# Decays in SBUF in a ring of five, with two state places, doubled PSUM banks and a joint silu trip, in the mix block of a two-layer kernel

## The chip, the core and the metric

The kernel runs on one core of a Trainium2 chip. The engines are PE (TensorE, matmuls), DVE (VectorE), ACT (ScalarE), POOL (GpSimd) and SP, which issues most of the DMAs. SBUF and PSUM are the core's memories; PE writes its sums to PSUM only. The metric is the device time of one execution in microseconds, less is better.

## The reference

Two layers on x of 8 sequences with 512 tokens of 256 channels. The first adds attention and a mixture of experts; the second, which is what the change touches, adds a state-space block (Mamba) and a linear layer on quantised data:

```python
xn = _layernorm(x, axis=-1)
x = x + _L1_attn_ref(xn, ...) + _L1_ffn_ref(xn, ...)

# _L1_attn_ref, per sequence, D_INNER 512, D_STATE 16
x, z = jnp.split(in_proj(hidden), 2, axis=-1)
u = jax.nn.silu(conv4(x) + conv1d_b)
dt_low, B_var, C_var = split(u @ x_proj_w.T)
delta = jax.nn.softplus(dt_low @ dt_proj_w.T + dt_proj_b)
dA = jnp.exp(delta[..., None] * A)
dBu = delta[..., None] * B_var[:, :, None, :] * u[..., None]
h = dA * h + dBu                      # over the 512 steps
y = einsum('bdn,bn->bd', h, c) + u * D_param
out = (y * jax.nn.silu(z)) @ out_proj_w.T

# _L1_ffn_ref: x and weight rounded to a 6 bit grid in blocks of 32
out = xd @ wd.T + bias
```

## The kernel before

Three blocks run one after another: `route_block` sends tokens to experts, `attend_block` does attention and experts, `mix_block` the second layer. The change is in `mix_block`, which occupies the last 1200 us.

There a sequence (a batch, b = 0 to 7) is cut into 32 **pieces**, numbered n over all batches, 256 in all. A piece is a quarter of the states of 64 channels on 128 partitions, laid out as two halves of 512 steps, so 1024 elements per partition. Eight pieces (`PER_CHUNK`) are one chunk of 128 channels. A piece n goes through four engines:

- ACT, `decay`: two exponentials of 512 elements (line 1333). They write into a **state place** in PSUM, `state(n)`, two banks; there are three places, used in turn. It waits until the read of piece n - 3 has emptied the place.
- POOL, `drive`: a product of 1024 elements, `rep` times `bc`, from SBUF into a ring `work` in SBUF with `WS` = 8 slots (line 1192). It waits until PE has summed the piece that was in the slot.
- DVE, `scan` (line 1460): a `tensor_tensor_scan` with the decay from PSUM and the drive from SBUF. It overwrites the decay with the states. Then `read` (line 1466) multiplies the states by C, back into the slot of `work`. DVE's order is scan n, side tasks, read n - 1.
- PE, `sum_states`: eight matmuls for each pair of pieces, into the bank `YB` of PSUM (line 1584). `seed` starts each chunk's sum with u * D, and waits until `gate_y` on DVE (line 1474) has multiplied the chunk before by silu(z) out of the same bank.

The order of all work is written by hand. Beside the pieces of batch b each engine has **side tasks** for the next batch f = b + 1, placed at piece numbers by the tables `PE_AT`, `ACT_AT`, `DVE_AT`, `POOL_AT`: the normalised tokens are turned, projected with four taps (line 1559) and passed through silu (1276), quantised by POOL and DVE (lines 1154, 1440, 1443, 1164, 1166, 1171), B, C and delta are made (1567, 1571, softplus 1304 and 1306), z is made (1552, silu 1314), and POOL forms the scans' inputs (1177, 1179), gathers the experts' outputs for batch b + 2 (1130) and adds them (1136). All side results pass through one PSUM bank, `TB`. The out-projection of batch b - 1 (1591 to 1595) stands among them at pieces 2 to 6. In the first batch they come `LATE` = 5 pieces later.

Every engine takes its instructions in this order, and a wait holds up all behind it. ACT must load a table whenever it changes between the functions exp, ln and silu (ACT_TABLE_LOAD). SP sends the delta and drive rows through HBM to have them copied across partitions (`store_inputs`, `load_inputs`, `load_quad`, `store_rows`).

Of the kernel before, what the change touches and what calls it, by code (L numbers as in the profile page):

```python
# [9 lines left out]
ALU = mybir.AluOpType  # L10
ACT = mybir.ActivationFunctionType
AX = mybir.AxisListType

P = 128
# [42 lines left out]
WS = 8  # L57
# [10 lines left out]
PE_AT = {"turn_x": (0, 1), "out": (2, 3, 5, 6), "w": 1, "first_quant": (2, 3), "x": (7, 9, 11, 13), "bc": 16, "dt": (18, 19, 20, 21),  # L68
         "z": (22, 23, 24, 25), "turn_quant": (26, 27)}
ACT_AT = {"normalise": 0, "turned": (1, 2), "out": (5, 8), "w": 2, "first_quant": (3, 4), "x": (10, 12, 14, 16), "silu_u": 16, "step": 9,  # L70
          "rows": 18, "dt": (19, 20, 21, 22), "softplus": 22, "z": (24, 25, 26, 27), "quant": (28, 29), "silu_z": 29, "weigh": 24}
DVE_AT = {"max": 2, "binade": 6, "statistics": 26}
POOL_AT = {"down": 9, "grid": 14, "up": 17, "gather": 23, "add": 27, "input": 28, "root": 31}
FIRST_ACT = {"weigh": 0}
# [855 lines left out]
def mix_block(nc, io, sb):  # L930

    with ExitStack() as ctx:
# [36 lines left out]
        work = buf("work3", [P, WS, 2, SEQ])  # L969
        absmax = buf("absmax", [P, TT * NBLK, 2])  # L970
# [4 lines left out]
        YB, TB = 6, 7  # L975
# [66 lines left out]

        def state(n):
            return ps[:, 2 * (n % 3):2 * (n % 3) + 2, :]

        with nc.Block() as block:
            @block.sync
            def _(sp):
# [49 lines left out]
                for b in range(BATCH + 1):  # L1098
                    if b < BATCH:
                        load_inputs(b, 1)  # L1100
# [3 lines left out]
                    if b < BATCH:  # L1104
                        load_inputs(b, 2)
# [3 lines left out]
                    if b < BATCH:  # L1109
                        load_inputs(b, 3)  # L1110
                    if b + 1 < BATCH:
                        store_rows(b + 1)
# [9 lines left out]
            def _(pool):  # L1122
# [90 lines left out]
                for b in range(BATCH):  # L1213
                    f = b + 1
                    for q in range(PIECES):
                        drive(b, q)
                        if b == 0:
                            if q == FIRST_POOL["add"]:
                                add_experts(1)
                            if q == FIRST_POOL["root"]:  # L1220
                                root(1)
                        if b + 2 < BATCH:
                            if q == POOL_AT["gather"]:
                                pool.drain()
                                place_gather(b + 2)
                                gather(b + 2, range(2))
# [551 lines left out]
```

## Time and profile before

| | us |
|---|---|
| median of 3 runs | 2224.48 (2223.17 to 2225.88) |
| profiled execution, its own time | 2220.31 |
| its span | 2218.5 |
| busy PE, DVE, ACT, POOL | 1719.3, 1488.8, 1004.6, 942.7 |

The span runs from the first instruction to the last. The mix block's pieces lie between 1128 and 2195 us of it. The profile's views used below are: busy time of the engines in a stretch (from:to, length, then busy us and count of instructions for PE matmul, PE weight load, DVE, ACT and POOL, the TensorE clock granted as a share, the DMAs' share, GB/s); groups of instructions by line (line, engine, operation, out<-in, partitions x elements, count | busy us, mean ns | idle us before them and who ended it); the waits (who waited <- for whom, us, times, longest); the timeline (start us, duration us, engine, line, operation, with equal neighbours merged as x2; in square brackets the idle time before and who ended it); and the durations of one line. An engine's instructions may overlap by some hundredths of a us.

### The profile page before, as it was taken

The numbers are of one execution on the slowest core, as the hardware profiler recorded it, in microseconds if no ns is written. First come the engines' busy times: TensorE is split into PE (matmuls) and PEld (weight loads), VectorE is DVE, ScalarE is ACT, GpSimd is POOL, SyncE is SP. The second block draws the span as 40 slices with busy tenths as digits, with TensorE's granted clock in tenths as the row PEclk, the third lists the DMA queues.
The fourth block names the chain that finished last, engine by engine and source line by source line (L and its number), as shares of the span: only waits on it lengthen the run. The fifth ranks groups of instructions, "written<-read, shape, count | busy, mean of one in ns | idle before, by whom it ended". The sixth has DMA issues, their size and how long they took to land.

```text
span 2218.5 us, 21659 instructions
## 1 busy us (share of the span) xinstructions
PE 1719.3 (77%) x6696; PEld 757.2 (34%) x6696; DVE 1488.8 (67%) x1744; ACT 1004.6 (45%) x1542; POOL 942.7 (42%) x676
## 2 busy tenths in 40 slices
PE   7499999999999999994727696685967859677645
PEld 7253535262625353531302141321413224132202
DVE  6446464546464646372068796987979888797995
ACT  3125252525343443434334746556465554656541
POOL 2700000000000000002288786877777877677761
PEclk9899999898989898997858796786977869777756
DMA  4553635262625354423141331423214142231420
GB/s 180 203 88 104 102 103 95 97 108 96 109 96 93 111 79 126 68 51 104 42 159 48 111 118 58 146 84 138 109 59 156 53 152 95 77 133 39 152 86 9
DMA packets 103055, 223.79 MB, mean 101 GB/s; under 512 B 12641, under 2 KB 64994, under 8 KB 99282
## 3 DMA queue, kind: packets, MB, share of 16 engines
q1 hardware_dynamic: 99922, 214.69, 34.1%
q0 software_dynamic: 3072, 8.37, 1.1%
q8 instruction: 28, 0.46, 0.1%
q14 instruction: 33, 0.27, 0.0%
HBM read 169.56 MB, written 53.48 MB: 101 GB/s over the span
## 4 chain that ended last, share of the span: by engine, by line
PE 18%; DVE 16%; issue 8%; ACT 8%; DVEq 1%; DMA 1%; POOLq 1%; POOL 1%; ACTq 0%; SPq 0%
DVE ps L1460 11%; PE ps L1559 9%; DVE work L1466 5%; PE ps L1584 3%; PE ps L1552 2%; ACT ps L1333 2%; PE ps L1571 2%; PE ps L1567 1%; ACT L1333 1%; ACT u L1276 1%; ACT inputs L1304 1%; ACT sz L1314 1%; ACT e_rows L1252 1%; PE ps L1591 0%; ACT L1306 0%
## 5 line engine op out<-in xcount | busy, mean ns | idle before, releaser
L1192 POOL TENSOR_TENSOR work<-rep,bc 128x1024 f32<-128x1024 f32 x256 | 600.2, 2365 | 166.2 <-PE ps L1584 143.1
L1460 DVE TENSOR_TENSOR_SCAN ps<-ps,work 128x1024 f32<-128x1024 f32 x256 | 585.2, 2286 | 119.5 <-ACT ps L1333 119.5
L1333 ACT ACTIVATE ps<-rep,a_neg 128x512 f32<-128x512 f32 x512 | 331.1, 682 | 311.9 <-DVE work L1466 310.1
L708 DVE TENSOR_REDUCE m<-ps 128x1 f32<-128x512 f32 x512 | 328.0, 686 | 158.8 <-PE ps L814 156.0
L631 ACT ACTIVATE prob<-ps 128x1024 f32<-128x1024 f32 x256 | 257.3, 1021 | 224.5 <-PE ps L838 222.7
L1584 PE MATMUL ps<-work,pick 128*32 128x512 f32 x1024 | 182.1, 792 | 180.7 <-DVE work L1466 180.7
L1466 DVE TENSOR_TENSOR work<-ps,bc 128x1024 f32<-128x1024 f32 x256 | 308.6, 1206 | 0.0
L572 POOL TENSOR_TENSOR m_parts<-m,nil 128x16 bf16<-128x16 f32 x32 | 7.0, 220 | 603.2 <-DVE m L708 603.2
L1559 PE MATMUL ps<-xn_t,in_taps 128*128 128x510 f32 (+3 forms) x512 | 232.4, 608 | 8.7 <-ACT x L1322 5.6
L814 PE MATMUL ps<-k_st,q_st 96*128 96x512 bf16 x512 | 200.3, 436 | 30.9 <-DVE m L708 24.7
L838 PE MATMUL ps<-q_st,k_st 99*128 99x512 bf16 x512 | 166.6, 423 | 1.0 <-DVE e_rest L684 0.3
L780 PE MATMUL ps<-rows_t,w 128*128 128x320 f32 x512 | 149.4, 440 | 4.3 <-ACT rows_t L609 4.3
L849 PE MATMUL ps<-prob,v 128*32 128x512 f32 x1024 | 147.5, 650 | 0.1
L1559 PEld LDWEIGHTS ps<-xn_t,in_taps 128*128 128x128 f32 x512 | 96.3, 193 | 146.0 <-issue 131.1
L1552 PE MATMUL ps<-xn_t,in_z 128*128 128x512 f32 x128 | 91.5, 858 | 55.2 <-ACT sz L1310 47.1
L789 PE MATMUL ps<-w,hid 128*128 128x256 f32 x512 | 120.8, 384 | 6.0 <-ACT hid_rest L613 6.0
L1584 PEld LDWEIGHTS ps<-work,pick 128*32 128x32 f32 x1024 | 22.6, 122 | 301.0 <-DVE work L1466 255.4
L586 POOL TENSOR_TENSOR att<-att,x_res 128x1024 f32<-128x1024 f32 x8 | 18.8, 2344 | 244.4 <-DVE att L693 244.4
L814 PEld LDWEIGHTS ps<-k_st,q_st 96*128 96x128 bf16 x512 | 50.2, 101 | 206.8 <-DVE m L708 168.2
L780 PEld LDWEIGHTS ps<-rows_t,w 128*128 128x128 f32 x512 | 97.4, 193 | 41.3 <-ACT rows_t L609 4.7
L680 DVE COPY e_out<-ps 128x256 f32<-128x256 f32 x32 | 12.0, 417 | 144.0 <-PE ps L789 144.0
L612 ACT ACTIVATE hid<-ps 128x256 f32<-128x256 f32 x128 | 49.0, 383 | 128.6 <-PE ps L780 128.6
(176 smaller groups left out, 2087.4 us busy)
## 6 DMA issues: line engine op xcount, KB each, us to landing
rep<-rep_rows SPq DMA_DIRECT2D x128, 512.0 KB, 6.1
w<-in_w SPq DMA_DIRECT2D x32, 1024.0 KB
bc<-bc_rows SPq DMA_DIRECT2D x32, 512.0 KB, 4.0
rep_rows<-inputs SPq DMA_DIRECT2D x32, 512.0 KB, 5.2
qk_parts<-parts SPq DMA_DIRECT2D x96, 128.0 KB
q_st<-qk_parts SPq DMA_DIRECT2D x96, 128.0 KB, 10.4
k_st<-qk_parts SPq DMA_DIRECT2D x96, 128.0 KB, 11.2
dispatch<-zeros SPq DMA_DIRECT2D x4, 1280.0 KB, 10.5
```

The costliest lines, as they stand in the source:

```text
L631: nc.scalar.activation(prob[:, n % PB, :, :], ps[:, ST[n % 2]:ST[n % 2] + 2, :], ACT.Exp, scale=SCALE).then_inc(prob_ready, 1)
L708: nc.vector.tensor_reduce(m[:, g % 2, qt, 2 * pair + i:2 * pair + i + 1], ps[:, S0 + i, :], AX.X, ALU.max).then_inc(s_reduced, 1)
L780: x = nc.tensor.matmul(ps[:, HIDE[i] + h % 2, 0:CAP], w1[:, i, k, h * P:(h + 1) * P], rows_t[:, k, :], start=(k == 0), stop=(k == KD - 1))
L814: nc.tensor.matmul(ps[:, S0 + i, :], q_st[0:STACK, h, qt * P:(qt + 1) * P], k_st[0:STACK, h, :], start=True, stop=True).then_inc(s_done, 1)
L838: x = nc.tensor.matmul(ps[:, ST[n % 2] + i, :], k_st[0:STACK + MROWS, h, kt * P:(kt + 1) * P], q_st[0:STACK + MROWS, h, :], start=True, st ...
L849: x = nc.tensor.matmul(ps[r * VW:(r + 1) * VW, PV, :], v[:, kt, g * GH + r, :], prob[:, (2 * k + r // 2) % PB, r % 2, :], start=(kt == 0), ...
L1192: nc.gpsimd.tensor_tensor(work[:, n % WS, :, :], rep[:, g % RS, 2 * h:2 * h + 2, 1, :], bc[:, k, 0, :].unsqueeze(1).broadcast_to([P, 2, SE ...
L1333: e = nc.scalar.activation(state(n)[:, i, :], rep[:, g % RS, 2 * h + i, 0, :], ACT.Exp, scale=a_neg[:, c, 2 * h + i, k:k + 1])
L1460: nc.vector.tensor_tensor_scan(s, s, work[:, n % WS, :, :].rearrange("p i t -> p (i t)"), 0.0, ALU.mult, ALU.add).then_inc(state_ready, 1)
L1466: nc.vector.tensor_tensor(work[:, n % WS, :, :], state(n), bc[:, k, 1, :].unsqueeze(1).broadcast_to([P, 2, SEQ]), ALU.mult).then_inc(read_ ...
L1559: x = nc.tensor.matmul(ps[:, bank, s:], in_x[:, k, TAPS - 1 - s, c * P:(c + 1) * P], xn_t[:, k, 0:SEQ - s], start=(s == 0 and k == 0), sto ...
L1584: x = nc.tensor.matmul(ps[j * CH:(j + 1) * CH, YB, :], pick[:, :], work[:, n % WS, i, :], start=False, stop=(n % PER_CHUNK >= PER_CHUNK - 2))
```

## The change

- `decay` writes into `decays` in SBUF, a ring of five pieces (`DS`), and waits for the scan of piece n - 5. `scan` reads both its inputs from SBUF and writes the states to PSUM, where there are now two places. It has a third wait, for the read of piece n - 2. `WS` goes from 8 to 7.
- `YB` and `TB` are two PSUM banks each. `seed` waits for the gating of the chunk before last; side tasks alternate between the banks.
- `gate_y` stands three pieces behind the start of the next chunk instead of one.
- silu of z for batch f - 1 follows directly on silu of u for batch f, under one table. The exponential of the softplus stands one piece ahead of its logarithm.
- Side tasks have new positions, written as chains that may begin before their batch (negative numbers); the out-projection moves to pieces 9 to 13, its copies to 15 and 18. SP loads the inputs of all chunks and stores the B and C rows ahead of the output's store.

```diff
-WS = 8
+WS = 7
+DS = 5
...
+GATE = 3
+PE_AT = {"turn_x": (-2, -1), "x": (1, 3, 5, 7), "bc": 11, "dt": (14, 15, 16, 17), "z": (18, 19, 20, 21), "turn_quant": (22, 23)}
+POOL_AT = {"down": 7, "grid": 14, "up": 17, "gather": -11, "add": -5, "input": 25, "root": -1}
+OUT_PROJ, OUT_COPY = (9, 10, 12, 13), (15, 18)
...
+        decays = buf("decays", [P, DS, 2, SEQ])
-        YB, TB = 6, 7
+        YB, TB = (6, 7), (4, 5)
...
+        def chains(n):
+            return [(f, n - (f - 1) * PIECES - (LATE if f == 1 else 0)) for f in range(1, BATCH)]
+
         def state(n):
-            return ps[:, 2 * (n % 3):2 * (n % 3) + 2, :]
+            return ps[:, 2 * (n % 2):2 * (n % 2) + 2, :]
...
                     if b < BATCH:
-                        load_inputs(b, 1)
+                        for c in range(1, DC):
+                            load_inputs(b, c)
+                    if b + 1 < BATCH:
+                        store_rows(b + 1)
...
-                    if n >= 3:
-                        act.wait_ge(read_ready, n - 2)
+                    if n >= DS:
+                        act.wait_ge(state_ready, n - DS + 1)
                     for i in range(2):
-                        e = nc.scalar.activation(state(n)[:, i, :], rep[:, g % RS, 2 * h + i, 0, :], ACT.Exp,
+                        e = nc.scalar.activation(decays[:, n % DS, i, :], rep[:, g % RS, 2 * h + i, 0, :], ACT.Exp,
                                                  scale=a_neg[:, c, 2 * h + i, k:k + 1])
...
+                        if at == ACT_AT["silu_u"]:
                             silu_u(f)
+                            if f > 1:
+                                silu_z(f - 1)
...
                     dve.wait_ge(drive_ready, n + 1)
+                    if n > 1:
+                        dve.wait_ge(read_ready, n - 1)
                     s = state(n).rearrange("p i t -> p (i t)")
-                    nc.vector.tensor_tensor_scan(s, s, work[:, n % WS, :, :].rearrange("p i t -> p (i t)"), 0.0,
-                                                 ALU.mult, ALU.add).then_inc(state_ready, 1)
+                    nc.vector.tensor_tensor_scan(s, decays[:, n % DS, :, :].rearrange("p i t -> p (i t)"),
+                                                 work[:, n % WS, :, :].rearrange("p i t -> p (i t)"), 0.0, ALU.mult, ALU.add).then_inc(state_ready, 1)
...
+                    if n > PER_CHUNK and (n - GATE) % PER_CHUNK == 0:
+                        c = (n - GATE) // PER_CHUNK - 1
+                        gate_y(c // DC, c % DC)
...
-                    if c or b:
-                        pe.wait_ge(y_ready, b * DC + c)
-                    nc.tensor.matmul(ps[:, YB, :], d_diag[:, c, :], u[:, (b * DC + c) % US, :], start=True, stop=False)
+                    if b * DC + c >= 2:
+                        pe.wait_ge(y_ready, b * DC + c - 1)
+                    nc.tensor.matmul(ps[:, YB[c % 2], :], d_diag[:, c, :], u[:, (b * DC + c) % US, :], start=True, stop=False)
```

How the order moves is seen at two places. The first is DVE at the seam of batch 0 and batch 1: before, with scans on line 1460 (printed as SCALAR_TENSOR_TENSOR), reads on 1466 and the gating on 1474:

```order
L1466 TENSOR_TENSOR work<-ps,bc 128x1024 [waits state_ready]
L1460 SCALAR_TENSOR_TENSOR ps<-ps,work 128x1024 [waits drive_ready,decay_ready]
L1474 TENSOR_TENSOR sz<-ps,sz 128x512 [waits z_taken,summed]
L1466 TENSOR_TENSOR work<-ps,bc 128x1024 [waits state_ready]
L1460 SCALAR_TENSOR_TENSOR ps<-ps,work 128x1024 [waits drive_ready,decay_ready]
L1430 TENSOR_REDUCE absmax<-xn 128x32 [waits quant_ready,xn_ready3]
```

The same place with the change, where scans are line 1468, reads 1474 and the gating 1482:

```order
L1468 SCALAR_TENSOR_TENSOR ps<-decays,work 128x1024 [waits read_ready,drive_ready,decay_ready]
L1436 TENSOR_REDUCE absmax<-xn 128x32 [waits quant_ready,xn_ready3]
L1474 TENSOR_TENSOR work<-ps,bc 128x1024 [waits state_ready]
L1468 SCALAR_TENSOR_TENSOR ps<-decays,work 128x1024 [waits read_ready,drive_ready,decay_ready]
L1440 TENSOR_SCALAR absmax<-absmax 128x32
L1442 RECIPROCAL inv_scale<-absmax 128x32
L1474 TENSOR_TENSOR work<-ps,bc 128x1024 [waits state_ready]
L1468 SCALAR_TENSOR_TENSOR ps<-decays,work 128x1024 [waits read_ready,drive_ready,decay_ready]
L1474 TENSOR_TENSOR work<-ps,bc 128x1024 [waits state_ready]
L1468 SCALAR_TENSOR_TENSOR ps<-decays,work 128x1024 [waits read_ready,drive_ready,decay_ready]
L1482 TENSOR_TENSOR sz<-ps,sz 128x512 [waits z_taken,summed]
```

The gating has moved from the second scan of the new batch behind its fourth, the block maxima stand two pieces earlier, and each scan reads `decays` and waits for `read_ready` too.

The second is ACT. Before, at the end of batch 0, the copies of z and of the quantised tokens end in silu of z (line 1314) with a table load on either side:

```order
L1310 ACTIVATE sz<-ps 128x512 [waits z_done] x2
L1318 ACTIVATE quant_t<-ps 128x512 [waits quant_turned] x2
L1314 ACT_TABLE_LOAD
L1314 ACTIVATE sz<-sz 128x2048
L1333 ACT_TABLE_LOAD [waits read_ready]
L1333 ACTIVATE ps<-rep,a_neg 128x512 [waits rep_loaded_0]
```

With the change silu of z (line 1319) comes in batch 1 behind the last projection of u and its silu (line 1279):

```order
L1273 ACTIVATE u<-ps,conv_b 128x512 [waits in_done]
L1279 ACT_TABLE_LOAD
L1279 ACTIVATE u<-u 128x1024 x2
L1319 ACTIVATE sz<-sz 128x2048
L1338 ACT_TABLE_LOAD
L1338 ACTIVATE decays<-rep,a_neg 128x512 [waits state_ready]
```

Silu of z has moved 14 pieces later (16 in the later batches), into the trip that silu of u makes anyway, and the decays (line 1338) wait for scans instead of reads.

## Rows read from the trace of the kernel before

**Rows 1.** Busy us by engine (count) in a stretch: one batch, the whole mix.
```profile
1422.00:1558.00 136.00, 99.10 (x312) 38.05 (x311) 115.30 (x82) 75.57 (x108) 104.45 (x60) 0.80 0.29 105
...
1126.00:2196.00 1070.00, 739.49 (x2329) 273.85 (x2329) 919.67 (x635) 573.45 (x824) 800.89 (x446) 0.77 0.28 100
```

**Rows 2.** Groups by line, mix: busy us, mean ns, idle before, releaser.
```profile
L1460 DVE TENSOR_TENSOR_SCAN ps<-ps,work 128x1024 f32<-128x1024 f32 x256 | 585.2, 2286 | 119.5 <-ACT ps L1333 119.5
```

**Rows 3.** Timeline, DVE, undisturbed pieces: start, us, engine, line, operation.
```profile
1302.06 2.28 DVE L1460 TENSOR_TENSOR_SCAN ps<-ps,work 128x1024 f32<-128x1024 f32 x1
1304.26 1.20 DVE L1466 TENSOR_TENSOR work<-ps,bc 128x1024 f32<-128x1024 f32 x1
1305.38 2.28 DVE L1460 TENSOR_TENSOR_SCAN ps<-ps,work 128x1024 f32<-128x1024 f32 x1
```

**Rows 4.** Waits in the mix: us in total, times, longest.
```profile
ACT ps L1333 <- DVE work L1466: 310.1, 154, 5.5
...
DVE sz L1474 <- PE ps L1584: 42.6, 20, 5.6
```

**Rows 5.** Timeline, first drive, first scan, last scan.
```profile
1128.19 6.95 POOL L1192 TENSOR_TENSOR work<-rep,bc 128x1024 f32<-128x1024 f32 x3 [2.47 <-DMA rep<-rep_rows]
...
1130.76 2.30 DVE L1460 TENSOR_TENSOR_SCAN ps<-ps,work 128x1024 f32<-128x1024 f32 x1 [19.25 <-ACT ps L1333]
...
2188.60 2.28 DVE L1460 TENSOR_TENSOR_SCAN ps<-ps,work 128x1024 f32<-128x1024 f32 x1
```

**Rows 6.** Groups by line, ACT in the mix.
```profile
L1314 ACT ACTIVATE sz<-sz 128x2048 f32<-128x2048 f32 x7 | 13.4, 1911 | 0.1
...
L1314 ACT ACT_TABLE_LOAD x7 | 9.0, 1283 | 0.5
```

**Rows 7.** Groups by line, POOL in the mix.
```profile
L1192 POOL TENSOR_TENSOR work<-rep,bc 128x1024 f32<-128x1024 f32 x256 | 600.2, 2365 | 166.2 <-PE ps L1584 143.1 <-DMA bc<-bc_rows 19.8 <-DMA rep<-rep_rows 2.5
L1177 POOL TENSOR_TENSOR inputs<-inputs 128x512 f32<-128x512 f32 x28 | 35.5, 1268 | 6.4 <-issue 6.0 <-ACT inputs L1306 0.4
...
L1130 POOL DMA_INDIRECT e_rows<-expert_out,slot_cur x24 | 23.8, 993 | 9.5 <-issue 7.7 <-PE ps L1584 1.8
...
L1144 POOL TENSOR_TENSOR rstd<-rstd,neg_half 128x4 f32<-128x4 f32 x7 | 7.3, 1049 | 1.3 <-issue 0.5
```

**Rows 8.** Timeline, two DVE operations that meet POOL's drives.
```profile
1291.97 5.17 POOL L1192 TENSOR_TENSOR work<-rep,bc 128x1024 f32<-128x1024 f32 x2
...
1294.26 0.68 DVE L1440 TENSOR_SCALAR e_rows<-xn 128x1024 int32<-128x1024 int32 x1
1295.02 2.67 DVE L1443 TENSOR_SCALAR e_rows<-e_rows 128x1024 f32<-128x1024 f32 x1
```

**Rows 9.** Single lines: xcount, duration ns min/median/max, first and last start.
```profile
L1192 POOL TENSOR_TENSOR work<-rep,bc x256: 2332/2352/2850, 1128.2 to 2172.6; 128x1024 f32<-128x1024 f32 x128
...
L1460 DVE TENSOR_TENSOR_SCAN ps<-ps,work x256: 2278/2285/2299, 1130.8 to 2188.6; 128x1024 f32<-128x1024 f32 x128
...
L1443 DVE TENSOR_SCALAR e_rows<-e_rows x8: 696/2674/2678, 1055.4 to 1977.4; 128x1024 f32<-128x1024 f32 x8
...
L1452 DVE TENSOR_TENSOR in_taps<-in_taps,work x4: 1210/1218/1485, 1039.0 to 1042.9; 128x1024 f32<-128x1024 f32 x4
```

**Rows 10.** Timeline, POOL's add and the first tap product on DVE.
```profile
1037.10 2.34 POOL L1136 TENSOR_TENSOR x<-x,e_rows 128x1024 f32<-128x1024 f32 x1 [6.50 <-ACT e_rows L1252]
...
1039.03 1.49 DVE L1452 TENSOR_TENSOR in_taps<-in_taps,work 128x1024 f32<-128x1024 f32 x1 [17.98 <-DMA rows_w<-in_fbias]
```

**Rows 11.** Timeline, POOL's indirect DMA issues beside DVE, earlier block.
```profile
85.65 0.97 POOL L81 DMA_INDIRECT dispatch<-xn_sb,slot_sb  x1 [0.31 <-issue]
...
85.75 0.73 DVE L657 STREAM_SHUFFLE e_out<-ps 128x512 f32<-128x512 f32 x1
...
86.58 1.23 DVE L659 TENSOR_TENSOR e_out<-e_out,sin 128x1024 f32<-128x1024 f32 x1
86.93 1.72 POOL L81 DMA_INDIRECT dispatch<-xn_sb,slot_sb  x1 [0.30 <-issue]
```

More of the change, by code:

```diff
@@ new lines, in _ @@
+                for n in range(BATCH * PIECES):
+                    drive(n // PIECES, n % PIECES)
+                    if n == FIRST_POOL["add"]:
+                        add_experts(1)
+                    if n == FIRST_POOL["root"]:
+                        root(1)
+                    for f, at in chains(n):
+                        if f > 1:
+                            if at == POOL_AT["gather"]:
+                                pool.drain()
+                                place_gather(f)
+                                gather(f, range(2))
+                            if at == POOL_AT["gather"] + 1:
+                                gather(f, range(2, TT))
+                            if at == POOL_AT["add"]:
+                                add_experts(f)
+                            if at == POOL_AT["root"]:
+                                root(f)
+                        if at == POOL_AT["down"]:
@@ L1356, in _ @@
                     take_dt(0, c, DT_FIRST[c])
+                exponents(0)
                 softplus(0)
                 act.wait_ge(a_ready, 1)
[L1359 to L1381 removed]
@@ new lines, in _ @@
+                for n in range(BATCH * PIECES):
+                    b, q = n // PIECES, n % PIECES
+                    decay(b, q)
+                    if n == FIRST_ACT["w"]:
+                        act.wait_ge(w_turned, 1)
+                        nc.scalar.activation(fw_t[:, :, :], ps[:, TB[0], :].rearrange("p (k d) -> p k d", d=DM), ACT.Copy).then_inc(w_copied, 1)
+                    for k in range(KD):
+                        if n == FIRST_ACT["quant"][k]:
+                            copy_quant(0, k, TB[1 - k])
+                    if n == FIRST_ACT["weigh"]:
+                        weigh_experts(1)
+                    for h in range(HALVES):
+                        if b and q == OUT_COPY[h]:
+                            copy_out(b - 1, h, TB[0])
+                    for f, at in chains(n):
+                        if f > 1 and at == ACT_AT["weigh"]:
+                            weigh_experts(f)
+                        if at == ACT_AT["normalise"]:
@@ L1399, in _ @@
                             softplus(f)
                         for c in range(DC):
[L1401 to L1402 removed]
+                            if at == ACT_AT["z"][c]:
+                                take_z(f, c, TB[1 - c % 2])
+                    if n == (BATCH - 1) * PIECES + ACT_AT["silu_u"]:
+                        silu_z(BATCH - 1)
+                    for f, at in chains(n):
                         for k in range(KD):
[L1404 to L1405 removed]
```

317 lines of the change are left out of this document (121 added, 196 removed).

## The prediction

> **What bounds the kernel now.** The change touches only the mix block, so I first cut the trace there. One middle batch (136 us) has DVE at 115.3, POOL at 104.5, PE at 99.1 and ACT at 75.6 us busy [rows 1]: DVE leads and POOL is 11 us behind it. The groups by line and the timeline say what DVE does: 256 scans of 2286 ns [rows 2], a read of 1.2 us behind each, and in a stretch that nothing disturbs scans start at 1302.06 and 1305.38, 3.32 us a piece [rows 3]. DVE is idle in two places: 119.5 us before scans for ACT's decays [rows 2], 19.2 of it before the very first scan [rows 5], and by the waits 42.6 us before the gating of y for PE's sums [rows 4]. Inside the loop that is 100.3 + 42.6 = 142.9 us. From the first scan's start at 1130.76 to the last one's end at 2188.60 + 2.28 = 2190.88 the loop takes 1060.1 us [rows 5]. So the loop is DVE's work plus 143 us of waiting. ACT's lateness has its own cause: its decays wait 310.1 us for DVE's reads [rows 4], because they are written into the three state places.
>
> **What the change takes away.** A decay now waits for the scan five pieces back instead of the read three back. The ring holds five pieces, 16.6 us at 3.32. ACT's longest trip becomes the joint one of the two silus: a load of 1.28, u in two parts of half the size of the 1.91 us pass over z, that pass, and a load back [rows 6], some 6.5 us. It fits, so I give the whole 100.3 us back. But silu of z now stands behind the decay of piece 45 (for batch 1), and DVE's gating behind scan 43 waits for it: that decay may start when scan 40 is done, and some 7.5 us of ACT stand against three pieces of DVE, 10 us. No cost as long as ACT uses its ring. Gating moves two pieces later, and its 42.6 us go too. The joint trip saves two table loads a batch, about 14 x 1.28 = 18 us of ACT, which is no bound: nothing on the path, since its decays are early anyway. Two PSUM banks for sums and two for side tasks shorten PE's waits for ACT and DVE. PE is 16 us a batch behind DVE, so zero, but for 0.7 us in the tail, where the out-projection waits for one copy. SP's new order moves stores and loads by some pieces. The waits for its loads in the loop fall on POOL before drives, in all 166.2 - 143.1 = 23.1 us of idleness that isn't PE's [rows 7], and cost DVE nothing now: its only waits are the two above. The drive ring of 7 instead of 8 takes one piece of lead from POOL: zero while POOL is the late one. ACT's exponentials now write SBUF; the pass over 2048 elements from SBUF to SBUF takes 1911 ns [rows 6], so a quarter of it at 682 ns or less: no cost.
>
> **What it adds: a small thing and a large one.** A scan now waits for the read issued just before it. Today it starts 0.08 us before that read ends (1304.26 + 1.20 = 1305.46 against 1305.38 [rows 3]). A drained start sits 0.08 us behind its predecessor (1294.94 to 1295.02 [rows 8]). So the wait costs 0 to 0.16 us, up to 41 us over 256 pieces, if DVE is the bound.
>
> By the Trainium skill ("VectorE: DVE Perf Modes", section "The DRAIN you can't avoid") a semaphore after each operation costs nothing extra. By that the term would be 0 instead of 41. The rows show a drain and an unwaited start, not this wait, so they don't settle it.
>
> The large one: the scan's first operand moves from PSUM to SBUF, so the scan reads two SBUF tensors. POOL spends its time on tensor operations with SBUF operands, 256 drives and seven kinds of others [rows 7]. What happens when such operations meet?
> 1. Today's scan, with one SBUF operand, doesn't disturb a drive: drives take 2332 at least and 2352 ns in the median, scans 2278 to 2299 [rows 9], and they overlap all the time.
> 2. Two DVE operations do collide with drives. The clamp of line 1443 takes 696 ns at its shortest but 2674 in the median of eight [rows 9]. At 1294.26 a DVE operation of 0.68 us comes in between two drives, and the two take 5.17 instead of 4.7. The second ends at 1297.14, which is 2.20 us after DVE has finished. DVE's next one ends at 1297.69, only 0.55 us after that drive [rows 8]. One runs, the other stands still, and the blocked one saves 0.15 us of start-up. These have one SBUF input and an SBUF output, so they are not quite the scan's shape.
> 3. The scan's shape on the reading side, two SBUF inputs, meets a POOL tensor operation once. The first tap product starts at 1039.03 while POOL adds until 1039.44 [rows 10], and takes 1485 against 1218 ns in the median of four [rows 9]. It ends at 1040.52, 1.08 us after POOL, again 0.14 less than a full run. It looks as if it had stood still until POOL was done.
> 4. The other way round: POOL's indirect DMA issue takes 0.97 us at 85.65, beside a shuffle that reads PSUM, and 1.72 us at 86.93, beside a DVE product of two SBUF inputs [rows 11].
>
> So I take scans and POOL's tensor operations as excluding each other for a whole operation.
>
> The Trainium skill states this ("SBUF — State Buffer", section "Who interferes with whom"): a DVE instruction with two SBUF inputs contends with a GpSimd instruction that reads SBUF, and whichever comes second is fully blocked. It speaks against this change: by it the sum is the one below, without it that of rival A. The trace agrees, with 1485 ns in place of 1218.
>
> **The sum.** What must then go one after the other:
> - 256 scans of 2.286 - 0.15 = 2.14: 548 us
> - 256 drives of 2.20: 563 us
> - POOL's other tensor operations: its 800.9 busy us [rows 1] less the drives' 600.2, the gather issues' 23.8 and the roots' 7.3 [rows 7] are 169.6, in 98 operations (28 each of two kinds, 14 and 4 x 7 of the quantiser and the adds) and some tiny ones; less 0.15 each: 155 us
> - the two DVE operations of item 2, seven times each: 14 x 0.55 = 8 us
>
> That is 1274. Scan and drive alternate, and the drive's 2.20 us covers the read's 1.2 and its new wait, so these and DVE's other work cost nothing more. The gathers and roots (31 us) and POOL's gaps (6.4 us before line 1177 alone [rows 7], say 14) lie beside scans if a drive is ready and beside nothing if not. I take half of the 45, 22 us: POOL has some 14 such operations a batch beside its 32 drives, so its lead is gone soon. That makes 1296 us from POOL's first drive at 1128.19 [rows 5], and the last scan ends near 2424. Behind the last scan come 2218.5 - 2190.9 = 27.6 us now, less 0.7: a span of 2451. The profiled run took 2220.31 for its span of 2218.5 (+1.8), and the median of the runs is 4.2 above it: **2457 us**, 232 more than 2224.5.
>
> The bounds of this case. Below: all 45 us hidden, and each drive letting go 0.1 us before its recorded end, about as much as a read and a scan overlap now: 2457 - 22 - 26 = 2409. Above: POOL's whole 800.9 us [rows 1] and the scans' whole 585.2 [rows 2] in a row, 1386, ninety more: 2547, and with POOL's gaps 2560.
>
> **Rivals.**
> *A, no exclusion, so faster.* The scan needs a new element only each 2.14 us / 1024 = 2.1 ns, and one meeting that cost 0.27 us is thin evidence for its shape. Then DVE stays the bound. It is busy 919.7 us in the mix stretch [rows 1]; with 0 to 41 us of new waits and 0 to 30 of left-over ones that makes 920 to 991 where 1064 stand (1130.8 to the last gating near 2195). The gain is 73 to 144, the middle 2115. Against it: items 3 and 4 are two unrelated delays, and the first has just the right size. 9%.
> *B, the two share their reads element by element.* A scan would take its second operand in half of its time and delay POOL by 256 x 1.07 = 274 us at most. POOL's 800.9 become 1075, with gaps up to 1110, against a stretch of 1070 now: 2225 to 2265. Against it: the clean ends in items 2 and 3. 5%.
> *C, exclusion as summed.* 86%. Should POOL's next operation overtake a waiting scan time and again, then DVE is later at first and POOL finds its ring full sooner; the operands are still never idle, and the sum holds.
> That the change doesn't do what it says is no rival: in the order every scan reads `decays,work`.
>
> **How the numbers follow.** The likeliest case gives 2457. A range of 2400 to 2560 holds nearly all of C, some 82% in all. Differences within 0.2% (4 us) count as no change, about what a measurement of this kernel can tell. Faster is A, 0.09; same is a sliver of B, 0.02; slower is C and the rest of B, 0.89.
>
> **What would show it.** Right: drives and scans far above 2352 and 2286 ns in their medians, up to 4.3 us for a blocked one; DVE's waits for decays down to the first 19 us; a batch of about 165 us; reads unchanged at 1.2. Wrong: scans still at 2286 and drives at 2352. Then A holds, and the gap before each scan gives the price of the new wait. If only drives are stretched, by about 1 us, it is B. If scans are stretched but a batch stays near 136 us, POOL's operations hold their operands for less time than I count, and what fails is the 2.20.

## The result: 13% slower, with scans and drives taking turns

The changed kernel takes 2518.03 us (median of 4 runs, 2515.25 to 2520.95) against 2225.18 for the kernel before, run beside it: a ratio of 1.1315 with a 95% interval of 1.1294 to 1.1336. The forecast was 2457 with a range of 2400 to 2560. The profiled execution took 2520.17 us, with a span of 2518.4. Line numbers have moved: drives are line 1199, scans 1468, reads 1474.

Busy time by engine in one middle batch and in the mix, changed kernel (columns as in [rows 1]):

```profile
1670.00:1844.00 174.00, 104.75 (x312) 38.72 (x312) 147.55 (x81) 72.91 (x107) 156.03 (x61) 0.71 0.25 82
1136.00:2492.00 1356.00, 753.81 (x2314) 273.10 (x2314) 1163.70 (x633) 558.65 (x812) 1226.27 (x446) 0.71 0.23 78
```

A batch has grown from 136 to 174 us, where some 165 were forecast. PE is busy for 104.8 instead of 99.1 us, at a granted clock of 0.71 instead of 0.80, and ACT for 72.9 instead of 75.6. DVE is busy for 147.6 instead of 115.3 us and POOL for 156.0 instead of 104.5, with as many instructions as before, give or take one. So no work was added. The instructions themselves got longer, and the groups by line say which:

```profile
L1468 DVE TENSOR_TENSOR_SCAN ps<-decays,work 128x1024 f32<-128x1024 f32 x256 | 787.2, 3075 | 135.8 <-POOL work L1199 86.7 <-ACT decays L1338 19.9
L1474 DVE TENSOR_TENSOR work<-ps,bc 128x1024 f32<-128x1024 f32 x255 | 306.5, 1202 | 0.0
...
L1440 DVE TENSOR_SCALAR absmax<-absmax 128x32 f32<-128x32 f32 x7 | 13.5, 1930 | 0.7
```

```profile
L1199 POOL TENSOR_TENSOR work<-rep,bc 128x1024 f32<-128x1024 f32 x256 | 875.6, 3444 | 92.5 <-PE ps L1584 89.0 <-DMA rep<-rep_rows 3.0 <-issue 0.2
...
L1184 POOL TENSOR_TENSOR inputs<-inputs 128x512 f32<-128x512 f32 x28 | 57.7, 2061 | 6.6 <-issue 6.6
...
L1137 POOL DMA_INDIRECT e_rows<-expert_out,slot_cur x24 | 39.3, 1636 | 9.5 <-issue 8.0 <-PE ps L1584 1.5
...
L1149 POOL TENSOR_TENSOR rstd<-moments,eps 128x4 f32<-128x4 f32 x7 | 13.0, 1862 | 2.7 <-DVE moments L1429 2.7
L1154 POOL TENSOR_TENSOR shift<-shift,rstd 128x4 f32<-128x4 f32 x7 | 12.0, 1721 | 1.0
L1131 POOL COPY slot_cur<-slot_sb 128x4 int32<-128x4 int32 x6 | 11.9, 1983 | 0.9 <-issue 0.2
```

Against [rows 2] and [rows 7]: a scan's mean went from 2286 to 3075 ns, a drive's from 2365 to 3444, while the read, which has one input in PSUM, still takes 1.2 us. POOL's sum of line 1184 (1177 before) went from 1268 to 2061, and the indirect DMA issue (1137, before 1130) from 993 to 1636. The last three rows are operations on 4 elements per partition.

The durations of the two lines (count, then minimum, median and maximum in ns), which answer to [rows 9]:

```profile
L1199 POOL TENSOR_TENSOR work<-rep,bc x256: 2332/4111/4375, 1136.7 to 2481.1; 128x1024 f32<-128x1024 f32 x128
L1468 DVE TENSOR_TENSOR_SCAN ps<-decays,work x256: 2299/3053/8980, 1139.3 to 2488.9; 128x1024 f32<-128x1024 f32 x128
```

The minimum is unchanged, 2332 for a drive. It is the meeting that costs. The timeline shows two meetings in a row (start, duration, engine):

```profile
1743.70 3.06 DVE L1468 TENSOR_TENSOR_SCAN ps<-decays,work 128x1024 f32<-128x1024 f32 x1
...
1744.76 4.14 POOL L1173 TENSOR_TENSOR xn<-xn,e_rows 128x1024 f32<-128x1024 f32 x1 [0.16 <-issue]
...
1746.67 1.20 DVE L1474 TENSOR_TENSOR work<-ps,bc 128x1024 f32<-128x1024 f32 x1
...
1748.01 3.05 DVE L1468 TENSOR_TENSOR_SCAN ps<-decays,work 128x1024 f32<-128x1024 f32 x1
...
1748.86 4.34 POOL L1199 TENSOR_TENSOR work<-rep,bc 128x1024 f32<-128x1024 f32 x1
```

The first scan ends at 1743.70 + 3.06 = 1746.76. POOL's operation on `xn` has been recorded since 1744.76 but ends at 1748.90, 2.14 us after the scan. The next scan starts at 1748.01 and ends at 1751.06, 2.16 us after that operation. The drive recorded from 1748.86 ends at 1753.20, 2.14 us after that scan. Read this way, one runs at each moment and the other stands. A scan and a POOL operation together need 1748.01 - 1743.70 = 4.31 us; the prediction had 2.14 + 2.20 = 4.34.

The waits (who waited for whom, us in total, times, longest) have changed too. Scans wait for decays only 19.9 us in the mix, as forecast, and the gating's waits are gone. In their place stand:

```profile
DVE ps L1468 <- POOL work L1199: 86.7, 33, 5.5
...
DVE stats L1422 <- POOL x L1143: 66.6, 6, 12.9
```

### The profile page after: what moved, and what is told of

Its sections match the earlier page's. It is cut to its first block, busy times and chain, and to the rows that moved or that the text cites. A ratio compares the mean times of both kernels' runs of the same rounds, so it can differ in the third digit from the quotient of the medians.

```text
span 2518.4 us, 21657 instructions
## 1 busy us (share of the span) xinstructions
PE 1743.7 (69%) x6696; PEld 760.1 (30%) x6696; DVE 1740.4 (69%) x1744; ACT 990.9 (39%) x1530; POOL 1368.3 (54%) x676
## 4 chain that ended last, share of the span: by engine, by line
DVE 20%; POOL 14%; POOLq 10%; issue 7%; PE 5%; ACT 2%; DVEq 1%; DMA 1%; ACTq 0%; SPq 0%
DVE ps L1468 12%; POOL work L1199 7%; DVE work L1474 5%; POOLq L1247 3%; POOLq L1169 3%; PE ps L1559 2%; POOL xn L1173 2%; POOLq L1185 2%; POOL e_rows L1137 2%; POOL xn L1171 1%; POOLq L1187 1%; POOLq L1176 1%; PE ps L1584 1%; POOL xn L1178 1%; POOL x L1143 1%
## 5 line engine op out<-in xcount | busy, mean ns | idle before, releaser
L1199 POOL TENSOR_TENSOR work<-rep,bc 128x1024 f32<-128x1024 f32 x256 | 875.6, 3444 | 92.5 <-PE ps L1584 89.0
L1468 DVE TENSOR_TENSOR_SCAN ps<-decays,work 128x1024 f32<-128x1024 f32 x256 | 787.2, 3075 | 135.8 <-POOL work L1199 86.7
L1338 ACT ACTIVATE decays<-rep,a_neg 128x512 f32<-128x512 f32 x512 | 339.7, 715 | 563.0 <-DVE ps L1468 542.0
L1584 PE MATMUL ps<-work,pick 128*32 128x512 f32 x1024 | 204.6, 885 | 475.0 <-DVE work L1474 475.0
L1559 PE MATMUL ps<-xn_t,in_taps 128*128 128x510 f32 (+3 forms) x512 | 250.4, 644 | 1.8 <-ACT xn_t L1269 1.0
L819 PE MATMUL ps<-k_st,q_st 96*128 96x512 bf16 x512 | 201.2, 438 | 35.5 <-DVE m L713 25.0
L1559 PEld LDWEIGHTS ps<-xn_t,in_taps 128*128 128x128 f32 x512 | 103.8, 208 | 157.5 <-issue 144.3
L785 PEld LDWEIGHTS ps<-rows_t,w 128*128 128x128 f32 x512 | 98.5, 195 | 42.6 <-ACT rows_t L614 4.7
L794 PEld LDWEIGHTS ps<-w,hid 128*128 128x128 f32 x512 | 95.1, 189 | 27.4 <-ACT hid_rest L618 11.2
```

Of the source, the lines that this page charges most:

```text
L785: x = nc.tensor.matmul(ps[:, HIDE[i] + h % 2, 0:CAP], w1[:, i, k, h * P:(h + 1) * P], rows_t[:, k, :], start=(k == 0), stop=(k == KD - 1))
L794: x = nc.tensor.matmul(ps[:, E_OUT[i], j * DM:(j + 1) * DM], hid[:, h, j * P:(j + 1) * P], w2[:, i, h, :], start=(h == 0), stop=(h == HC - 1))
L819: nc.tensor.matmul(ps[:, S0 + i, :], q_st[0:STACK, h, qt * P:(qt + 1) * P], k_st[0:STACK, h, :], start=True, stop=True).then_inc(s_done, 1)
L1199: nc.gpsimd.tensor_tensor(work[:, n % WS, :, :], rep[:, g % RS, 2 * h:2 * h + 2, 1, :], bc[:, k, 0, :].unsqueeze(1).broadcast_to([P, 2, SE ...
L1338: e = nc.scalar.activation(decays[:, n % DS, i, :], rep[:, g % RS, 2 * h + i, 0, :], ACT.Exp, scale=a_neg[:, c, 2 * h + i, k:k + 1])
L1468: nc.vector.tensor_tensor_scan(s, decays[:, n % DS, :, :].rearrange("p i t -> p (i t)"), work[:, n % WS, :, :].rearrange("p i t -> p (i t) ...
```

## The experiments

The theory: a scan with two SBUF inputs and a POOL operation with SBUF inputs exclude each other, and that is the whole loss. The rival at first: the new order, or the scan's new wait for the read ahead of it, makes part of the loss. Each time below is compared with the kernel before, run in the same sitting.

### One operand back in PSUM

Made from the changed kernel. All order, waits and transfers stay, but the scan takes its first operand from PSUM:

```diff
-tensor_tensor_scan(s, decays[...], work[...], 0.0, ALU.mult, ALU.add)
+tensor_tensor_scan(s, s, work[...], 0.0, ALU.min, ALU.max)
```

> The changed kernel in which the scan reads its first operand from its own PSUM state place instead of the ring in SBUF; ACT still writes the ring, and every order, wait and ring size stays. The scan computes a minimum and a maximum instead of product and sum, on stale values, so the states are not the reference's. Theory (a scan with two SBUF inputs and a POOL operation with SBUF inputs exclude each other): scans back at 2286 ns, drives at 2352 in the median, DVE the bound again, loop from first drive to last scan 920 to 1000 us instead of 1354, time 2080 to 2170. Rival (the new order, the ring of 7, two places or the read wait cost the time): loop stays above 1300 us and the time above 2450.

Measured: 2222.02 us (2219.42 to 2229.98), ratio 0.9993 (0.9974 to 1.0013). Groups by line, and then the durations of drives:

```profile
L1468 DVE TENSOR_TENSOR_SCAN ps<-ps,work 128x1024 f32<-128x1024 f32 x256 | 588.4, 2298 | 58.0 <-ACT decays L1338 19.9 <-POOL work L1199 5.0
```

```profile
L1199 POOL TENSOR_TENSOR work<-rep,bc x256: 2334/2355/2810, 1133.2 to 2179.8; 128x1024 f32<-128x1024 f32 x128
```

Scans are at 2298 again, drives at 2355 in the median and never above 2810. The operand's place is the whole difference to the changed kernel, 296 us. But 2080 to 2170 was missed: without the exclusion the new schedule gains nothing. The timeline of an undisturbed stretch shows one reason:

```profile
1584.92 1.21 DVE L1474 TENSOR_TENSOR work<-ps,bc 128x1024 f32<-128x1024 f32 x1
1586.26 2.30 DVE L1468 TENSOR_TENSOR_SCAN ps<-ps,work 128x1024 f32<-128x1024 f32 x1
1588.47 1.21 DVE L1474 TENSOR_TENSOR work<-ps,bc 128x1024 f32<-128x1024 f32 x1
1589.81 2.30 DVE L1468 TENSOR_TENSOR_SCAN ps<-ps,work 128x1024 f32<-128x1024 f32 x1
```

A read ends at 1584.92 + 1.21 = 1586.13, and the scan that waits for it starts 0.13 us later. Before, it started 0.08 us ahead of the read's end [rows 3]. Scans stand 1589.81 - 1586.26 = 3.55 us apart instead of 3.32: 0.23 us a piece, 59 us over 256. The second reason is a new wait of DVE, and the third a 128x32 operation on DVE that now meets POOL's drives:

```profile
DVE stats L1422 <- POOL x L1143: 65.5, 6, 12.1
```

```profile
L1440 DVE TENSOR_SCALAR absmax<-absmax x8: 183/1962/1968, 1056.0 to 1963.4; 128x32 f32<-128x32 f32 x8
```

The statistics of the next batch wait 65.5 us in six places until POOL has added the experts' outputs. Line 1440 takes 1962 ns in the median instead of 183, about 11 us over seven batches; the long ones start while a drive is under way and end 0.04 us behind its end. DVE's 920 busy us of the mix, plus 59, 65.5 and 11, make 1056; the loop from first to last scan took 1059. So most of the given-back 143 us is spent again.

### The ring alone, in the kernel before

The kernel before with the decays in SBUF and the drive ring of 7, and nothing else of the change: its own order, three state places, its banks, its silus. Since the decays no longer show that a state place is free, the scan waits for the read that empties it, three pieces back.

```diff
-WS = 8
+WS = 7
+DS = 5
...
-                    if n >= 3:
-                        act.wait_ge(read_ready, n - 2)
+                    if n >= DS:
+                        act.wait_ge(state_ready, n - DS + 1)
...
+                    if n > 2:
+                        dve.wait_ge(read_ready, n - 2)
-tensor_tensor_scan(s, s, work[...], ...)
+tensor_tensor_scan(s, decays[:, n % DS, ...], work[...], ...)
```

> The kernel before with one part of the change: decays in a ring of five in SBUF, drive ring of 7, state places still three, and everything else in the old order. Theory: the exclusion alone makes the loss; what must go one after the other is the same 1274 us, with POOL's small operations on top as in the changed kernel: 2480 to 2560. Rival (the new order makes a good part of it): below 2400.

Measured: 2513.16 us (2 runs, 2511.04 and 2515.28), ratio 1.1302 (1.1274 to 1.1329), as slow as the whole change.

```profile
L1194 POOL TENSOR_TENSOR work<-rep,bc 128x1024 f32<-128x1024 f32 x256 | 879.4, 3458 | 74.1 <-PE ps L1588 66.2 <-DMA bc<-bc_rows 4.2 <-DMA rep<-rep_rows 3.0
L1464 DVE TENSOR_TENSOR_SCAN ps<-decays,work 128x1024 f32<-128x1024 f32 x256 | 842.6, 3292 | 155.6 <-ACT decays L1335 120.2 <-issue 35.5
```

Drives take 3458 ns and scans 3292 in the mean, over 1350 us from first drive to last scan. The 35.5 us without a releaser are waits for drives as well: these scans start 0.09 us behind a drive's end. This part makes the loss by itself, and DVE waits 120.2 us for decays besides. That these waits are there here and gone in the changed kernel, with the same time, suggests that such waiting costs little while POOL is at work, since its operations have to run alone anyway.

### The read wait alone, in the kernel before

```diff
                     dve.wait_ge(drive_ready, n + 1)
+                    if n > 1:
+                        dve.wait_ge(read_ready, n - 1)
```

> The kernel before with one wait more: each scan waits for the read issued just before it. It prices that wait where DVE is the bound. By the rows of the drained start it costs 0.16 us a piece, some 168 of them undisturbed, and less where the scan waits for ACT anyway: 20 to 41 us more, 2245 to 2266. Rival (a wait on a semaphore costs nothing): within 5 us of 2225.

Measured: 2242.04 us (2239.46 to 2247.24), ratio 1.0085 (1.0061 to 1.0109), a little less than the 2245 to 2266 expected and clear of the rival.

```profile
L1462 DVE TENSOR_TENSOR_SCAN ps<-ps,work 128x1024 f32<-128x1024 f32 x256 | 588.4, 2298 | 132.8 <-ACT ps L1333 101.6 <-DVE work L1468 0.5
```

A scan takes 2298 instead of 2286 ns, and pieces are 3.55 us apart, as in the first experiment. Of the 59 us that this makes at most, 47 are there in the loop: DVE is busy 16 us longer and stands 31 us in the new gaps. Only 18 show in the time, because slower pieces let the others catch up: waits for decays fall from 119.5 to 101.6, those of the gating from 42.6 to 31.3. By the Trainium skill ("VectorE: DVE Perf Modes", section "The DRAIN you can't avoid") a semaphore behind each of eight tensor_copy operations costs nothing extra. Here one between a read and a scan costs 0.23 us in undisturbed pieces, and the measurement decides.

### What in the drive excludes the scan

Two changed kernels in which the drives do less. In the first they only write, in the second they have one SBUF input:

```diff
-tensor_tensor(work[:, n % WS, ...], rep[...], bc[...], ALU.mult)
+memset(work[:, n % WS, :, :], 0.25)                        # first
+tensor_copy(work[:, n % WS, ...], rep[...])                # second
```

> The changed kernel in which each drive is a memset of the same 1024 elements, which writes SBUF and reads nothing (left out: the product). It takes about 0.99 us instead of 2.35, so the time falls either way, to 2080 to 2170 with DVE as bound. What tells is the duration of the scans: if only POOL's reads exclude them, the median scan is 2286 ns and memsets stay at 1.0 us even where they overlap a scan; only the scans that meet POOL's other operations are longer. Rival (any SBUF operation of POOL excludes a scan): memsets that meet a scan take 2 to 3 us.

> The changed kernel in which each drive is a copy from SBUF to SBUF of the same 1024 elements, one input instead of two (the product is left out). A copy takes about 1.04 us alone. With e4_drives_write it tells whether one SBUF input is enough for the exclusion. Theory: yes, so copies that meet a scan take up to 3 us and scans that meet a copy about 3.2, where 205 of 256 scans were at 2.30 us beside memsets. Rival (only POOL's operations with two inputs exclude a scan): copies stay at 1.04, and scans at 2.30 except beside POOL's other operations.

The first took 2215.61 us, the second 2289.37 (one run each; the kernel before 2223.92 and 2223.74). Durations of drives and scans, first kernel:

```profile
L1199 POOL MEMSET work<- x256: 941/951/1492, 1133.5 to 2171.1; 128x1024 f32 x128
L1467 DVE TENSOR_TENSOR_SCAN ps<-decays,work x256: 2298/2300/4393, 1136.1 to 2183.9; 128x1024 f32<-128x1024 f32 x128
```

Of the 256 fills 101 lie wholly inside a scan, 59 of them inside scans that took no longer than 2.31 us; the 101 take 951 ns in the median, 976 at most. Scans are at 2300. Writing alone excludes nothing. Only POOL's other operations, which read SBUF, still stretch a scan:

```profile
1596.57 3.26 POOL L1173 TENSOR_TENSOR xn<-xn,e_rows 128x1024 f32<-128x1024 f32 x1 [0.16 <-issue]
...
1598.92 3.06 DVE L1467 TENSOR_TENSOR_SCAN ps<-decays,work 128x1024 f32<-128x1024 f32 x1
...
1600.66 0.95 POOL L1199 MEMSET work<- 128x1024 f32 x1 [0.83 <-PE ps L1583]
1601.77 1.93 POOL L1178 TENSOR_TENSOR xn<-xn,absmax 128x1024 f32<-128x1024 f32 x1 [0.16 <-issue]
...
1603.22 2.63 DVE L1467 TENSOR_TENSOR_SCAN ps<-decays,work 128x1024 f32<-128x1024 f32 x1
...
1603.64 0.95 POOL L1199 MEMSET work<- 128x1024 f32 x1
```

The fill at 1600.66 runs inside the scan at 1598.92. That scan is long, 3.06 us, because of POOL's operation of line 1173, which ends at 1599.83, 2.15 us before the scan does. The scan at 1603.22 is recorded with 2.63 and ends 2.15 us after the product of 1601.77. The second kernel:

```profile
L1199 POOL COPY work<-rep x256: 1028/1174/3076, 1131.6 to 2245.5; 128x1024 f32<-128x1024 f32 x128
L1467 DVE TENSOR_TENSOR_SCAN ps<-decays,work x256: 2299/2300/4264, 1134.2 to 2258.3; 128x1024 f32<-128x1024 f32 x128
```

Of the 256 copies 158 take 1.03 to 1.2 us, but 50 take 2.8 to 3.08, nearly a scan's time more, and scans reach 4264. One SBUF input on POOL's side is enough. The Trainium skill ("SBUF — State Buffer", section "Who interferes with whom") says so of a GpSimd instruction that reads SBUF and excepts one that only writes; both kernels agree. The first kernel's time missed its forecast of 2080 to 2170. Its trace has the same reasons as the first experiment, up to 59 us of read waits and 41.8 of waiting for the statistics' input, and a third: POOL's other operations still stretch its scans, by 43 us in all against 2298 ns each.

### The statistics later

The changed kernel, with the statistics behind POOL's add instead of three pieces ahead of it:

```diff
-"statistics": -8
+"statistics": -5
```

> The changed kernel with DVE's statistics three pieces later (5 instead of 8 before the batch), so that DVE no longer waits 66.6 us at six places for POOL's add of the experts. Theory A (what both engines need in turn is the bound, and DVE's waiting only shifts work within it): that wait goes to below 15 us but the time falls by less than 10 us. Theory B (during that wait POOL runs small operations and gathers that use the operands little, so the wait is part of the time missing in the sum): the time falls by 20 to 60 us, to 2460 to 2500.

Measured: 2510.92 us (2509.34 to 2511.93), 7 us less than the changed kernel, ratio 1.1281 (1.1261 to 1.13) to the kernel before. The two ratios' intervals touch, and 3 of the 7 us lie ahead of the first drive (1133.63 against 1136.71). The waits:

```profile
DVE ps L1468 <- POOL work L1199: 117.8, 50, 5.5
...
DVE stats L1422 <- POOL x L1143: 22.4, 5, 4.5
```

The wait for the add falls by 44 us, to 22.4 and not below 15 as expected. The waits for drives grow by 31. A DVE wait is nearly free here as well, since POOL goes on meanwhile.

### Without the gathers

The changed kernel without POOL's gathers and the small copies ahead of them for the batches from 2 on (the experts' outputs are left out of them). ACT's weighing of the rows, which waited for the gathers, there waits for POOL's last quantiser operation instead:

```diff
                            if at == POOL_AT["gather"]:
-                                pool.drain()
-                                place_gather(f)
-                                gather(f, range(2))
-                            if at == POOL_AT["gather"] + 1:
-                                gather(f, range(2, TT))
+                                pass
```

> The changed kernel without POOL's gathers of the experts' outputs and the two small copies ahead of them for batches 2 to 7 (left out: those outputs, so stale rows are added). They take 39.3 + 11.9 + 1.1 us of POOL there, more than half of it waiting for scans. Theory (small POOL operations that wait out a scan each, and leave the operands idle afterwards, are what the sum lacked): 30 to 70 us less, 2450 to 2490. Rival (the bound is the big operations alone): within 15 us of 2518.

Measured: 2486.83 us (2486.19 and 2487.48), 31 us less. The loop takes 1325.3 instead of 1354.4 us. The time in which neither a scan nor a tensor operation of POOL (512 elements or more) is under way is 45 us instead of 70.5. So the gathers do lie beside nothing to a large part: their 39.3 busy us, with the copies of 4 elements, cost 31.

### A version that gains

Without the ring, what DVE waits for can be shortened in other ways. From the kernel before, first the gating one piece later, then the exponential of the softplus a piece ahead of its logarithm too:

```diff
-                        if b and q == 1:
+                        if b and q == 2:
...
-                            if q == PER_CHUNK * (c + 1) + 1:
+                            if q == PER_CHUNK * (c + 1) + 2:
```
```diff
-"softplus": 22
+"softplus": 23
...
+                        if q == ACT_AT["softplus"] - 1 + late:
+                            exponents(f)
```

> The kernel before with the gating of y one piece later, behind the third scan of the next chunk instead of the second; decays stay in PSUM with three places. DVE's 42.6 us of waiting there should fall below 10 us; the seed of the next chunk, which waits for the gating, comes one piece later in DVE's time but stands at the same place in PE's order. Theory: 20 to 38 us less, 2185 to 2205. Rival (PE's sums come later instead, and POOL and DVE wait for them): within 5 us of 2224.

> The kernel of v1_gate with one thing more: the exponential of the softplus a piece ahead of its logarithm, nothing else moved. It shows which half of v3_apart gave something. DVE waits 42.1 us at piece 23 in v1_gate. Theory: the trip at that place is 1.9 us shorter and stands behind one more decay, 10 to 25 us less than v1_gate, 2181 to 2196. Rival (the waits move): within 5 us of 2206.

The first takes 2205.82 us (2203.5 to 2206.59), ratio 0.9908 (0.9891 to 0.9926), about 1% less and just above the 2185 to 2205 expected:

```profile
DVE ps L1460 <- ACT ps L1333: 141.8, 37, 19.5
...
DVE sz L1474 <- PE ps L1584: 2.6, 2, 2.1
```

The gating's waits fall from 42.6 to 2.6 us, but half of that comes back as waits for decays, 141.8 instead of 119.5: DVE is ahead sooner. The second takes 2200.37 us (2199.3 to 2203.4), ratio 0.9892 (0.987 to 0.9915). That is the lowest time of all kernels here, but its 2181 to 2196 were missed, and the ratios' intervals of the two overlap:

```profile
DVE ps L1465 <- ACT ps L1335: 129.5, 46, 19.8
```

At the piece of the softplus the waits fall from 42.1 to 13.7 us, and 14.8 of it come back one piece on. Two more kernels contain both changes and more; the first of them was run before the second kernel above, and is compared with the first in what was expected. One moves silu of u and all side tasks behind it a piece later, the other also puts silu of z ahead of the copies of the quantised tokens:

```diff
-"silu_u": 16, ... "dt": (19, 20, 21, 22), "softplus": 23, "z": (24, 25, 26, 27), "quant": (28, 29), "silu_z": 29
+"silu_u": 17, ... "dt": (20, 21, 22, 23), "softplus": 24, "z": (25, 26, 27, 28), "quant": (29, 30), "silu_z": 30     # one
+"silu_u": 17, ... "quant": (30, 31), "silu_z": 29     # the other
```

> The kernel of v1_gate with ACT's two long trips cut: the exponential of the softplus a piece ahead of its logarithm, silu of u a piece behind the last copy of u, and all that follows in the batch one piece later. DVE waits 5.6 us at piece 17 and 7.1 at piece 23 of a batch for decays in the kernel before, 76 us over six batches. A trip is 1.9 or 0.6 us shorter, and starts behind another decay. Theory: half or more of the 76 us goes on top of the gain of v1_gate, 2130 to 2175. Rival (ACT has three places whatever the order, so the waits only move to other pieces): like v1_gate.

> The kernel of v3_apart with silu of z one piece earlier, directly behind the last copy of z, and the two copies of the quantised tokens behind it, so that this trip doesn't stand next to the normalising of the next batch. In v3_apart DVE waits 44.9 us at the first piece of a batch (19 of it before the first scan). Theory: 10 to 20 us less than v3_apart, 2185 to 2196. Rival: within 5 us of 2206.

They take 2206.39 (ratio 0.992, 0.9895 to 0.9946) and 2203.88 us (0.9907, 0.9886 to 0.9929): no gain over the other two, and both far from the 2130 to 2175 and 2185 to 2196 expected. For both the rival holds: waits moved, among others to piece 0 of the next batch, 44.9 and 47.3 us there (some 20 of them before the very first scan) instead of 28.8.

## Why the prediction was right, and where it was short

**Exclusion, and the sum: right.** A pair takes 4.31 us against 4.34. Over the loop, scans and POOL's tensor operations cover 1283.9 us of time, all records laid over one another; the forecast was 1274. The experiments with the operand in PSUM and with the ring alone show that this is the change's whole loss. That 2518 lies within the range is in part luck. The upper end, 2547 to 2560, came mostly from leaving out the saved start-up, and the pairs show that it is saved; what filled the room was idle time that no bound had above 45 us.

**Case C's overtaking: right.** POOL's next operation can pass a waiting scan:

```profile
1609.66 6.95 POOL L1199 TENSOR_TENSOR work<-rep,bc 128x1024 f32<-128x1024 f32 x3
...
1612.10 6.68 DVE L1468 TENSOR_TENSOR_SCAN ps<-decays,work 128x1024 f32<-128x1024 f32 x1 [3.39 <-POOL work L1199]
```

The first of the three drives ends near 1611.98 and the scan is recorded from 1612.10, but the two other drives go ahead of it. They end at 1616.61, the scan at 1618.78, 2.17 us later. Six scans are longer than 6 us in this way, the longest 8980 ns, 13445 in the kernel with the ring alone. As said, the operands are not idle meanwhile.

**The steps that failed: "half of the 45", and "the drive's 2.20 us covers the read's 1.2 and its new wait".** The time from POOL's first drive at 1136.71 to the last scan's end at 2491.15 is 1354.4 us; the forecast was 1296. Ten of the 58 missing are the sum's. The other 48 are time in which neither a scan nor one of POOL's tensor operations is under way: 70.5 us, where 22 were allowed. Sorted by what POOL does in that time, it has two parts.

The first part, 46.8 us, is what the prediction had counted as 45 and put beside scans by half: 26.2 at the gathers and the copies ahead of them, 9.2 at the roots and the 4-element operation behind them, 11.4 at the other small fills and gaps. So as much time as all of it, and not half, lies beside nothing. Two gathers show how:

```profile
1430.60 2.30 DVE L1468 TENSOR_TENSOR_SCAN ps<-decays,work 128x1024 f32<-128x1024 f32 x1 [2.10 <-POOL work L1199]
1430.67 3.04 POOL L1137 DMA_INDIRECT e_rows<-expert_out,slot_cur  x1 [0.16 <-issue]
1432.81 1.21 DVE L1474 TENSOR_TENSOR work<-ps,bc 128x1024 f32<-128x1024 f32 x1
1434.01 0.94 POOL L1137 DMA_INDIRECT e_rows<-expert_out,slot_cur  x1 [0.30 <-issue]
```

The scan ends at 1432.90 and the first gather only at 1433.71; the second follows, and the next drive starts at 1434.98. In these 2.07 us DVE does its read and then waits. The 4-element operations of lines 1149 and 1154 take 1862 and 1721 ns in the same way, where 202 was usual, and the index copy 1983 for 183. That lengthening lies beside a scan and costs nothing by itself, but it puts the small work that follows behind the scan's end. Behind it POOL's next drive is late, and the scan behind that waits in turn: of waits for drives there are 86.7 us that were not there before. The kernel without gathers has 25 us less of idle time, close to the 26.2.

The second part, 22.3 us in 20 places, the prediction had at nothing. There POOL's drive waits for PE to sum the piece in its slot, so it doesn't cover the read:

```profile
1508.84 2.79 DVE L1468 TENSOR_TENSOR_SCAN ps<-decays,work 128x1024 f32<-128x1024 f32 x1
1511.55 1.20 DVE L1474 TENSOR_TENSOR work<-ps,bc 128x1024 f32<-128x1024 f32 x1
...
1512.88 2.30 DVE L1468 TENSOR_TENSOR_SCAN ps<-decays,work 128x1024 f32<-128x1024 f32 x1
...
1513.98 3.35 POOL L1199 TENSOR_TENSOR work<-rep,bc 128x1024 f32<-128x1024 f32 x1 [4.50 <-PE ps L1584]
```

POOL has stood for 4.50 us, and from the scan's end at 1511.63 to the next one's start at 1512.88 the read stands alone, 1.25 us. Whether a drive ring of 8 would have avoided this was not tried. The 1.4 us left are mostly the read before the last scan.

**A start that moved by 8.5 us.** The first drive came at 1136.71 instead of 1128.19. It lies behind the attention block, which the change doesn't touch. The other kernels' first drives came between 1127.4 and 1133.6, with the ones made from the changed kernel at 1131.6 and later. What shifts it was not tried. With the 58 us this is the 67 between a span of 2451 and 2518.4. The 27.6 us behind the last scan became 27.25 where 26.9 were forecast.

**The read wait: too small, and nearly without effect here.** "0 to 0.16 us a piece" was 0.23. In the changed kernel it stands beside a drive, as the step said, but for 30 stretches of the idle time that end in a scan 0.13 us behind its read. At 0.21 us each that is 6 us, an estimate. In the kernel before it costs 18 us, in the kernel with its operand in PSUM up to 59.

**Waits given back: right in kind, wrong in worth.** Decays come in time, 19.9 us of waits are left, all at the start, and the gating doesn't wait. But "I give the whole 100.3 us back" and rival A's 2115 overlooked that the new positions put the statistics three pieces ahead of POOL's add: 66.6 us of new waits in six places. Had A held, the kernel would have stood near 2222, no change, and not 2115. The tables held that: `"add"` stands at -5 for POOL, `"statistics"` at -8 for DVE.

**No cost: right for two, open for one.** Silu of z ahead of the gating and PE's banks show no new wait on DVE. That the drive ring of 7 is free isn't shown: drives wait for their slots in the 20 places above.

## What to carry to other kernels

Before an operand is moved from PSUM to SBUF, count the SBUF inputs of the DVE instruction that reads it: with two, as in this kernel, its time adds to that of every POOL operation that reads SBUF, and the sum of the two is the new bound, however well they overlapped. Where two engines exclude each other, price their common time as a union of records. Add to it every small operation and gap of the one as time beside nothing, and the other's short work between two long operations wherever the first may be waiting for a buffer. When a wait is removed, follow each side task of the waiting engine to its own producer, since the engine arrives there earlier.

## What was new of the hardware

- A POOL operation on 4 elements that reads SBUF waits out a scan with two SBUF inputs: 1.7 to 2.0 us in the mean for 0.2 (lines 1149, 1154 and 1131).
- POOL's fill of 1024 elements doesn't exclude the scan (951 ns inside one), its copy with one input does (1.03 to 3.08 us).
- An indirect DMA issue on POOL is stretched by such scans from 993 to 1636 ns.
- A DVE operation that waits for the one just ahead of it on the same engine starts 0.13 us behind its end, where one without that wait starts 0.08 us before it. With a scan 12 ns longer, that is 0.23 us a piece.
- A DVE operation that stands blocked can be passed by POOL operations that start after it: one in the scans of 6.7 us, two in that of 9.0, four in those of 12.4 and 13.4 in the kernel with the ring alone.
